# Four attention and feed-forward layers on one core: every engine's loops written out, and two ScalarE copies placed ahead of an exponential

## What is computed

```python
x = x + L0_xattn(layernorm(x), ctx)   # 8 heads of 128
x = x + L0_ffn(layernorm(x))          # 9 ternary experts, gates of top 1
x = x + L1_xattn(layernorm(x), ctx)   # 16 heads of 8, with biases
x = x + L1_ffn(layernorm(x))          # piecewise linear gelu, rounded
x = x + L2_xattn(layernorm(x), ctx)   # 16 heads of 64
x = x + L2_ffn(layernorm(x))          # masked by an argmax
x = x + L3_xattn(layernorm(x), ctx)   # 16 heads of 64
x = x + L3_ffn(layernorm(x))          # gated experts, top 2
# an attention:
q, k, v = heads(x @ Wq), heads(ctx @ Wk), heads(ctx @ Wv)
out = softmax(scale * q @ k.T) @ v    # per sequence and head
return merge(out) @ Wo + bo
```

## Time and profile before

| what | value |
|---|---|
| median of 3 runs | 3998.56 us (3996.25 to 4007.36) |
| the profiled execution | 3976.25 us, span 3974.5 us |
| instructions | 110071, of them 44952 matmuls and 44952 weight loads |
| PE busy | 3612.0 us, 91% of the span |
| DVE, ACT, POOL busy | 62%, 46%, 28% |
| granted TensorE clock, mean | 0.929 |
| instruction fetches (queue q8) | 305 packets, 5.00 MB |

### The profile page before, as it was taken

The page is one execution under the profiler, slowest core; times in us unless marked ns, Lnnn a source line. Parts: engine busy times, 40 slices in busy tenths (PEclk is TensorE's granted clock), DMA queues, the critical chain, the costliest instruction groups (busy, mean ns, idle before and its releaser), DMA issues. The chain is left out here.

```text
span 3974.5 us, 110071 instructions
## 1 busy us (share of the span) xinstructions
PE 3612.0 (91%) x44952; PEld 3024.5 (76%) x44952; DVE 2445.7 (62%) x5145; ACT 1821.4 (46%) x3060; POOL 1102.7 (28%) x814
## 2 busy tenths in 40 slices
PE   4999599998989788699999989979999997999999
PEld 3888588886778654488878867768788886888888
DVE  5777555554444499766665657656566665666665
ACT  2555355554444455355555545445455552332322
POOL 1222133334333133222222213312222221222222
PEclk9999799997576599899999989989999998999999
DMA  1000000000000000000000000010000001000000
GB/s 69 11 10 6 25 0 0 0 0 18 9 11 9 8 0 0 23 6 8 6 8 6 6 10 0 0 26 6 9 6 7 8 4 32 1 11 11 0 11 11
DMA packets 14677, 39.22 MB, mean 10 GB/s; under 512 B 3148, under 2 KB 4748, under 8 KB 12813
## 3 DMA queue, kind: packets, MB, share of 16 engines
q1 hardware_dynamic: 14341, 33.97, 2.7%
HBM read 29.77 MB, written 4.19 MB: 9 GB/s over the span
## 5 line engine op out<-in xcount | busy, mean ns | idle before, releaser
L536 ACT ACTIVATE projL<-bank 128x512 f32<-128x512 f32 (+1 forms) x640 | 373.6, 604 | 716.2 <-PE bank L135 700.6
L359 POOL TENSOR_TENSOR probL<-probL,invL 128x1024 f32<-128x1024 f32 x160 | 304.7, 1905 | 1274.2 <-DVE invL L618 1274.2
L1162 POOL TENSOR_TENSOR accM<-accM,partM 128x512 f32<-128x512 f32 x272 | 348.0, 1279 | 817.1 <-DVE partM L1264 815.7
L1235 ACT ACTIVATE siluM<-bank 120x512 f32<-120x512 f32 x240 | 143.7, 599 | 457.3 <-PE bank L135 457.1
L440 PEld LDWEIGHTS bank<-valuesL,probTL 64*64 64x64 f32 x10240 | 282.2, 134 | 69.0 <-issue 54.3
L440 PE MATMUL bank<-valuesL,probTL 64*64 64x128 f32 x10240 | 321.2, 275 | 13.1 <-ACT probTL L546 13.1
L1184 PEld LDWEIGHTS bank<-downT,hM 120*128 120x128 f32 x2560 | 310.5, 192 | 15.0
L615 DVE TENSOR_REDUCE totalL<-probL 128x16 f32<-128x1024 f32 x160 | 194.9, 1218 | 199.4 <-ACT probL L551 199.2
L1184 PE MATMUL bank<-downT,hM 120*128 120x128 f32 x2560 | 311.5, 275 | 0.0
L607 DVE TENSOR_REDUCE neg_maxL<-bank 128x16 f32<-128x1024 f32 x160 | 196.0, 1225 | 186.7 <-PE bank L459 142.4
L1184 PEld LDWEIGHTS bank<-w2T,hM 128*128 128x128 f32 x2304 | 276.1, 192 | 38.5 <-ACT hM L1238 21.6
(11 more groups left out here) (263 smaller groups left out, 8463.4 us busy)
## 6 DMA issues: line engine op xcount, KB each, us to landing
ct0L<-in_ctxP SPq DMA_DIRECT2D x24, 192.0 KB, 2.4
ct1L<-in_ctxP SPq DMA_DIRECT2D x24, 192.0 KB, 3.0
x<-in_x SPq DMA_DIRECT2D x4, 1024.0 KB, 9.0
out<-x SPq DMA_DIRECT2D x4, 1024.0 KB, 3.9
nct<-in_ctxP SPq DMA_DIRECT2D x16, 192.0 KB, 2.4
w_natural<-in_L0w SPq DMA_DIRECT2D x2, 1152.0 KB, 8.9
downT<-in_L3down SPq DMA_DIRECT2D x1, 1200.0 KB, 12.8
gateT<-in_L3gate SPq DMA_DIRECT2D x1, 900.0 KB, 4.8
```

What stands on the lines that cost most here:

```text
L359: nc.gpsimd.tensor_tensor(segments(prob[:, slot, :]), segments(prob[:, slot, :]), per_segment(inv[:, slot, :]), ALU.mult).then_inc(prob_re ...
L536: nc.scalar.activation(proj[:, u, :], rot.bank(step, f"P{u}")[0:rows, :], ACT.Copy, scale=scale if paired and u % 2 == 0 else 1.0).then_in ...
L1162: nc.gpsimd.tensor_tensor(acc[:, :, :], acc[:, :, :], part[:, ex % 2, :, :], ALU.add)\
```

## The change

Every `Fori` of the eight stages becomes a Python `for`, so each engine's program of a stage is emitted in full, with constants as wait targets and addresses. The groups follow in the same order with the same slots. Besides, in A1 the ACT program does `keep_q` and `keep_output` of step k=2 ahead of that step's exponential, where they stood behind it. No other instruction of any engine's data work is moved, added or dropped; the register instructions and the jumps back are gone.

```diff
-def sweep(engine, group):
-    group(0, 0, True)
-    with engine.Fori(0, NG // 2 - 1) as j:
-        group(2 * j + 1, 1, False)
-        group(2 * j + 2, 0, False)
-    group(NG - 1, 1, False)
+def sweep(group):
+    for j in range(NG):
+        group(j, j % 2, j == 0)
...
-                    with dve.Fori(q * NG // 4, (q + 1) * NG // 4) as i:
+                    for i in range(q * NG // 4, (q + 1) * NG // 4):
...
-    with sp.Fori(1, NG // 2) as m:
+    for m in range(1, NG // 2):
...
-        def sweep_from_two(engine, group):
-            group(0, 0)
-            group(1, 1)
-            with engine.Fori(1, NG // 2) as j:
-                group(2 * j, 0)
-                group(2 * j + 1, 1)
+        def straight(group):
+            for j in range(NG):
+                group(j, j % 2)
...
-        def groups(engine, group):
-            group(0, 0, 0)
-            group(1, 1, 1)
-            with engine.Fori(1, NG // 2 - 1) as j:
-                group(2 * j, 0, j)
-                group(2 * j + 1, 1, j + 1)
-            group(NG - 2, 0, NG // 2 - 1)
-            group(NG - 1, 1, None)
+        def straight(group):
+            for j in range(NG):
+                group(j, j % 2, (j + 1) // 2 if j + 1 < NG else None)
...
                             keep_probs(m - 2, 1)
+                        if k == 2 and more:
+                            keep_q(i + 1)
+                        if k == 2 and started(i, 1):
+                            keep_output(i - 1)
                         if k or started(i, 1):
                             exponentials(m - 1, (k - 1) % 2)
                         if k == 0 and more:
                             keep_transposed(nc, act, c, xt_bank, i + 1, 1 - slot, xt_done, xT_ready)
                         if k == 1 and more:
                             keep_k(i + 1, 1 - slot, t_bank[0])
-                        if k == 2 and more:
-                            keep_q(i + 1)
-                        if k == 2 and started(i, 1):
-                            keep_output(i - 1)
```

More of the change, by code:

```diff
@@ L369, in _ @@
                 group(0, 0)
-                with pool.Fori(1, NG // 2) as j:
+                for j in range(1, NG // 2):
                     group(2 * j - 1, 1, j)
@@ L503, in group @@
                         scores(m, i, slot, k)
-                sweep_from_two(pe, group)
+                straight(group)
                 for n in (NS - 2, NS - 1):
@@ L570, in group @@
                         keep_value(m, 2, step)
-                sweep_from_two(act, group)
+                straight(group)
                 exponentials(NS - 1, 1)
@@ L657, in group @@
                             add_output(i - 1)
-                sweep_from_two(dve, group)
+                straight(group)
                 maxima(NS - 1, 1)
@@ L783, in _ @@
                 pool.wait_ge(bias_ready, 1)
-                groups(pool, group)
+                straight(group)
                 add_bias(NG - 2)
@@ L927, in _ @@
                 pe.wait_ge(bias_ready, 1)
-                groups(pe, group)
+                straight(group)
                 for n in (NS - 2, NS - 1):
@@ L1002, in _ @@
                 keep_v(0, 0, t_bank[1])
-                groups(act, group)
+                straight(group)
                 exponentials(NS - 1, 1)
@@ L1061, in group @@
                             finish(i - 2)
-                groups(dve, group)
+                straight(group)
                 add_output(NG - 2)
@@ L1163, in group @@
                             .then_inc(added, 1)
-                sweep(pool, group)
+                sweep(group)
             @block.tensor
@@ L1216, in group @@
                             transpose_group(nc, pe, c, xr_bank, i + 1, xh_ready, xt_done)
-                sweep(pe, group)
+                sweep(group)
                 for n in range(2):
@@ L1247, in group @@
                             keep_transposed(nc, act, c, xr_bank, i + 1, 1 - slot, xt_done, xT_ready, affine)
-                sweep(act, group)
+                sweep(group)
             @block.vector
@@ L1309, in group @@
                     ch.close()
-                sweep(dve, group)
+                sweep(group)
                 for n in range(3):
@@ L1551, in _ @@
                 nc.gpsimd.memset(shift[:, 1:2], -QUARTER + 0.25).then_inc(shift_set, 1)
-                with pool.Fori(0, NG) as i:
+                for i in range(NG):
                     for n in range(N):
```

## The result

The changed kernel takes 3826.14 us, the median of four executions (3801.25 to 3867.66), against 3997.4 us (3994.05 to 4007.36) for the kernel before: a ratio of 0.9547, with a 95% interval of 0.9485 to 0.9609. That is 4.5% faster, inside the range given, and 40 us above the point. The execution at 3867.66 us was disturbed and is left out of the ratio; the median of the other three is 3814.12 us.

A forecast was written before the change was run, and what follows sets the result against it. TensorE bounds the kernel, with stalls at jumps back and a low clock in A1. Gains 71.9 + 120.8 + 5 + 2.3 = 200 us off 3976.25 give 3776, taken as 3786 on the median's scale; range 3753 to 3880.

The forecast's parts named there:

- the point: Whole kernel: the forecast time of 3786 us, given chance 0.60.
- the rival by which a group boundary costs this anyway: A2 and A3: any group boundary stalls, so straight code changes nothing there; 3858 us, chance 0.04.
- each stall is also followed by a stretch at the lower level: TensorE's jumps back: slow matmuls follow each stall; included in the 71.9 us gain of A2 and A3.
- the clock holds: A1: long waits go, so all groups run at full clock, 264.0 us in place of 384.81, 120.8 us less.
- The group's price: A1: a full-clock group takes 19.2 us in place of 20.19, as the copies move ahead of the exponential.
- the clock falls now and then: A1: a third to two thirds of groups at the lower clock, 54 to 107 us back; 3840 to 3893, chance 0.20.
- the tail: End of A1: 19.07 us of TensorE work at clock 0.50 shrinks by 0 to 9.5 us, taken as 5.
- the slower rival: A0, F0, F1, F2, F3: 153 new fetches stall TensorE at 3.58 us each, 548 us; 4334 us, chance 0.04.
- some 450 fetches: Whole kernel: instruction fetches rise from 305 by some 153, at about 98 matmuls a fetch, costing 0.
- the terms: F1: VectorE's stage, each jump back leaves a wait of 0.4 us, 2.3 us gained in all.
- the 22.3 us difference: Whole kernel before: median 3998.56 us above the profiled execution; the forecast 3786 lies between 3776 and 3798.

The follow-up runs named there:

- four fillers: Changed kernel plus four 128x128 identity matmuls a group, result unread, ahead of TensorE's wait at step k=3 in A1: 3760.18 us, ratio 0.9435.
- F1 with 14: Changed kernel plus unread identity matmuls ahead of TensorE's waits, 8 a group in A1 and 14 a group in F1: 3784.98 us, ratio 0.948.
- one at the starts of A2 and A3: Changed kernel with 4 unread matmuls a group in A1, plus 64 ahead of the weights' wait starting A2 and A3: 3768.92 us, ratio 0.945.
- the run with the delaying copies: Changed kernel with 8 unread matmuls a group at A1's k=1, plus two 128x128 ScalarE copies ahead of k=2's exponential: 3839.34 us, ratio 0.9626.

## Why the prediction was right, and where it was off

**A2 and A3: right, term and mechanism.** 30.2 and 43.0 us against 30.5 and 41.4; the run with these loops alone written out gives 30.0 and 40.5. The stall at a jump back is the cost, no other comes in its place, and the rival by which a group boundary costs this anyway is out. The Trainium skill's price for a branch (about 108 ns) is not what decides here. Another page of the Trainium skill bears on it: "Runtime: NRT & Kernel Launch", section Instruction fetch mechanics, says that a taken branch whose target is outside the small window of code an engine keeps has to fetch it first. The traces agree in kind: no wait and 8 fetches in F3 with two groups in the body, 0.8 and 1.1 us and 37 fetches with four. The size differs from A2's 3.58 us, and why one costs more than the other is open. So is why A3's jumps cost more (4.6 to 5.1 us) than A2's; in the records of before two fetches start within 0.9 us of each other as each of A3's six stalls begins (3117.3 and 3117.9 us at the fifth) and none do at A2's, six fetches more in all, which points at a cause and proves none. One reading in the prediction was too wide: "each stall is also followed by a stretch at the lower level" holds for eleven of the twelve, and the 3.58 us one at 1925.2 has none.

**A1: the step "the clock holds" failed.** The sum took 13.75 groups at 19.2 us, 264.0; they took 336.2, so the term gave 48.6 us and not 120.8. The group's price was good (18.6 to 18.8 measured at full clock, with a gap of 0.6 to 1.3 us ended by the exponential, as forecast), but the groups were not all at full clock. The step rested on the 1.86 us wait of the earlier trace rows that was survived, and on falls only at waits of about 2 us. Of the five falls three came at waits of 0.93 to 1.26 us, one at 0.58 and one at none, and one wait that was survived shows no bound: 1.07 was survived too and 0.93 was not. Once low, the level stayed there for 27 to 92 us, but for the first time (6.8 us), although TensorE then waits for nothing, which the earlier trace rows had shown. That is the rival "the clock falls now and then", to which I gave 0.20 and 3840 to 3893; 3826 lies between it and the forecast. With four fillers the clock holds, the 55 steps take 262.2 us (forecast 264.0) and A1 takes 341.5; the forecast was 465.6 - 125.8 = 339.8. So 76 of the 77.7 us that A1 fell short go with the clock. A second term of A1 failed with it: the tail was to give 5 us and gave nothing, 26.7 us from the last step's scores to the stage's end before and after, with the clock low all through it.

**Loading: a missed term.** I put register instructions at 0 and had no term for this stage. Here they and the jump back are on VectorE's chain; the rows of VectorE show it, first before, then after.

```profile
7.95 0.06 DVE L150 MEMSET spacer<- 128x1 f32 x1 [0.25 <-issue]
...
9.91 0.06 DVE L150 MEMSET spacer<- 128x1 f32 x1 [0.23 <-issue]
```

```profile
6.97 0.29 DVE L149 BATCH_NORM_STATS2 bn<-x 128x6 f32<-128x128 f32 x1
...
8.38 0.29 DVE L149 BATCH_NORM_STATS2 bn<-x 128x6 f32<-128x128 f32 x1
```

A pass of 1.96 us became one of 1.41, 0.55 us by 16 passes, 8.8 of the 9.9 us. How much of it is the registers and how much the jump, no run tells. I had looked only at stages in which TensorE is the bound; here nothing hides VectorE. That the forecast of the whole is not further off is in part luck: A1 fell 77.7 us short of the sum, and loading with some us in F3, F1 and A3 brought back 16 that it didn't count on.

**Fetches: the price right, the count wrong.** No looped stage stalls when written out (F0 +0.7, F2 0, F3 -2.1 us), so the slower rival is out. But I forecast some 450 fetches and there are 356. The 274 of before in A1, A2 and A3 did not stay: written out these stages need 236, since a loop that stalls fetches more than straight code. And the other stages went from 31 to 120, 89 more and not 153: 125 matmuls to a fetch, where I had worked with 98.

**F1:** -4.2 for -2.3. The jumps' 0.4 us each are gone, as in the terms; the rest is open. It is no more than what falls of the clock move here: F1 has four of 3.4 us in the changed kernel, and the same code took 294.1 and 297.3 us in different runs.

**From the profiled time to the median.** I took half of the 22.3 us difference. The executions of the changed kernel order themselves by clock: 3801.25 at 0.956, 3814.12 at 0.950, 3838.15 at 0.943, so the spread within a kernel goes with the clock. With fillers the scatter shrinks (3757.99 to 3774.31 against 3801.25 to 3838.15).

## What to carry to other kernels

Write a loop out where its timeline shows a wait for "issue" at the jump back, and price it as the pairs without a jump times their number: here that was right to 2 us. Where TensorE's clock falls and stays low, look for the short wait in front of each fall, also one of 1 us, and count a gap that is made shorter as mended only when it is gone or filled; a few products whose result nobody reads, no longer than the wait, gave 54 us here (3814.12 to 3760.18; 45 by the two ratios, each taken against the kernel before on its own chip). Try it on the stage: here neither the length of a wait nor a count of matmuls alone told where the level falls. A filler longer than its wait costs time, as F1 with 14 showed, and one at the starts of A2 and A3 gained nothing.

## What the runs showed of the hardware

- In A1 the granted clock fell from 2.4 to 1.2 GHz behind waits of TensorE as short as 0.93 us, and at twelve of fifteen waits of 1.12 to 1.14 us in the run with the delaying copies; at 0.73 us, fourteen in a row, never. I had looked for waits of 2 us. These lengths are no bounds: single falls came at 0.58 and 0.68 us, three at no wait over 0.35 us, and eleven of fourteen waits of 2.0 to 2.2 us in F1 and one of 3.58 us in A2 had none.
- A busy TensorE doesn't raise the level soon: 92.2 us at 1.2 GHz in the changed kernel with no wait over 0.3 us in them. What raises it again, and why it fell at 1173.3 us without a wait, is open. In the run with 1.12 us waits it came back after 7 to 20 us, which isn't explained either.
- The Trainium skill ("TensorE: Matmul & The Clock Gate", section Part 4: PE-mode transpose) has transposes not count as work for the clock in the way matmuls do. A1, in which they are 5.6 of a group's 17.6 us of TensorE work, holds 2.4 GHz for 290 us with four fillers, so among this much other work they don't stand in the way; a stretch of transposes alone was not run.
- A loop's jump back costs nothing on TensorE in F0, F2, F3 and A0, 0.8 and 1.1 us with F3's body doubled, and 3.1 to 5.1 us in A1, A2 and A3. Where it costs nothing the loop's stage has few instruction fetches (F3 8, A0 10); where it stalls it has more than the same stage written out (F3 with the doubled body 37 for 33, A2 93 for 82, A3 99 for 82).
